# The down product of a row tile in one 512-column bank, and its adapter columns in a bank of their own

## What is computed

```python
def lora_add(base, inp, A, B):
    Ab = A[layer_idx][lora_indices]
    Bb = B[layer_idx][lora_indices]
    t = jnp.einsum('bri,bni->bnr', Ab, inp)
    return base + jnp.einsum('bor,bnr->bno', Bb, t) * SCALE
gate = lora_add(jnp.einsum('bnh,fh->bnf', x, W_gate), x, A_gate, B_gate)
up = lora_add(jnp.einsum('bnh,fh->bnf', x, W_up), x, A_up, B_up)
act = jax.nn.silu(gate) * up
down = lora_add(jnp.einsum('bnf,hf->bnh', act, W_down), act, A_down, B_down)
x = x + down          # H = 512, F = 1376
```

## Times and profile before

| | us |
|---|---|
| median of three runs | 654.25 |
| lowest, highest | 652.68, 658.75 |
| the profiled execution, from its first to its last instruction | 656.1 |

### The profile page before, as it was taken

The page is one execution under the profiler, slowest core; times in us unless marked ns, Lnnn a source line. Parts: engine busy times, 40 slices in busy tenths (PEclk is TensorE's granted clock), DMA queues, the critical chain, the costliest instruction groups (busy, mean ns, idle before and its releaser), DMA issues.

```text
span 656.1 us, 11454 instructions
## 1 busy us (share of the span) xinstructions
PE 615.8 (94%) x4659; PEld 599.5 (91%) x4659; DVE 300.1 (46%) x748; ACT 202.5 (31%) x514; POOL 210.0 (32%) x230
## 2 busy tenths in 40 slices
PE   4798998999999999999998999899987999999997
PEld 4797998999899899999998999899987998898985
DVE  3576543243333333333233323332331346889897
ACT  3464422231223122313231323132311333333331
POOL 4348341114111501151115111511164512656551
PEclk9899999999999989999999899999997999999998
DMA  6775042114212411141124011401134111131212
GB/s 201 251 257 160 30 136 85 39 34 131 75 39 65 126 47 39 65 141 33 39 65 157 17 39 65 157 17 39 33 129 129 39 33 49 50 97 65 96 49 81
DMA packets 26613, 55.80 MB, mean 85 GB/s; under 512 B 4224, under 2 KB 7744, under 8 KB 26560
## 3 DMA queue, kind: packets, MB, share of 16 engines
q1 hardware_dynamic: 18608, 31.17, 14.0%
q0 software_dynamic: 7808, 23.86, 12.0%
q10 hardware_dynamic: 144, 0.03, 0.0%
HBM read 46.66 MB, written 8.39 MB: 84 GB/s over the span
## 4 chain that ended last, share of the span: by engine, by line
PE 79%; DVE 9%; issue 6%; POOL 2%; ACT 1%; DMA 1%; SPq 1%; POOLq 0%; DVEq 0%; ACTq 0%
PE gu_ps L1031 15%; PE gu_ps L1030 15%; PE gu_ps L1029 15%; PE down_ps L1030 7%; PE down_ps L1029 7%; PE down_ps L1031 7%; DVE route L930 2%; PE l_ps L1031 2%; PE l_ps L1029 2%; PE l_ps L1030 2%; DVE x L948 1%; DVE wgu_sb L881 1%; POOL a_raw L563 1%; PE x2t_ps L1137 1%; PE tg_ps L1029 1%
## 5 line engine op out<-in xcount | busy, mean ns | idle before, releaser
L1029 PE MATMUL gu_ps<-xt,wgu_sb 128*128 128x256 f32 (+1 forms) x704 | 203.2, 289 | 9.3 <-DVE wgu_sb L881 8.3
L1031 PE MATMUL gu_ps<-xt,wgu_sb 128*128 128x256 f32 (+1 forms) x704 | 202.9, 288 | 5.0 <-issue 4.7
L1030 PE MATMUL gu_ps<-xt,wgu_sb 128*128 128x256 f32 (+1 forms) x704 | 202.5, 288 | 3.2 <-issue 3.1
L857 DVE TENSOR_TENSOR act<-act,gu_ps 128x256 f32<-128x256 f32 (+1 forms) x88 | 37.0, 420 | 243.2 <-ACT act L681 238.0
L1029 PEld LDWEIGHTS gu_ps<-xt,wgu_sb 128*128 128x128 f32 (+1 forms) x704 | 136.5, 194 | 11.6 <-DVE wgu_sb L881 8.3
L1031 PEld LDWEIGHTS gu_ps<-xt,wgu_sb 128*128 128x128 f32 (+1 forms) x704 | 136.8, 194 | 5.7 <-issue 5.7
L1030 PEld LDWEIGHTS gu_ps<-xt,wgu_sb 128*128 128x128 f32 (+1 forms) x704 | 136.5, 194 | 2.0 <-issue 2.0
L563 POOL DMA_INDIRECT b_sel_raw<-b_gu,idx_rank x48 | 46.2, 963 | 259.5 <-PE gu_ps L1031 243.6
L681 ACT ACTIVATE act<-gu_ps 128x256 f32<-128x256 f32 (+1 forms) x88 | 33.7, 383 | 289.8 <-PE gu_ps L1031 223.9
L1029 PE MATMUL down_ps<-wd_sb,act_hl 128*128 128x288 f32 (+1 forms) x352 | 104.8, 298 | 3.4 <-POOL wd_sb L625 1.9
L1031 PE MATMUL down_ps<-wd_sb,act_hl 128*128 128x288 f32 (+1 forms) x352 | 104.3, 296 | 2.8 <-issue 2.8
(11 more groups left out here) (132 smaller groups left out, 1019.1 us busy)
## 6 DMA issues: line engine op xcount, KB each, us to landing
wgu_sb_raw<-wgu SPq DMA_DIRECT2D x20, 256.0 KB, 5.2
xt_raw<-x_t SPq DMA_DIRECT2D x16, 256.0 KB, 3.1
x_res<-x_rows SPq DMA_DIRECT2D x8, 512.0 KB
x_after_l<-x_res SPq DMA_DIRECT2D x8, 512.0 KB
x<-x_after_l SPq DMA_DIRECT2D x16, 256.0 KB
out<-y SPq DMA_DIRECT2D x15, 256.0 KB, 2.1
wd_sb_raw<-wd SPq DMA_DIRECT2D x10, 256.0 KB, 5.6
w_raw<-w2ra_t SPq DMA_DIRECT2D x1, 1296.0 KB
```

The source lines that it names most:

```text
L857: ve.tensor_tensor(act[0:k, s % 2, :], act[0:k, s % 2, :], gu_ps[s % GU_BANKS][0:k, 1, :], ALU.mult).then_inc(s_mul, 1)
L1029: pe.matmul(out_, stationary[0], moving[0], start=start, stop=False, skip_group_check=True)
L1030: pe.matmul(out_, stationary[0], moving[1], start=False, stop=False, skip_group_check=True)
L1031: return pe.matmul(out_, stationary[1], moving[0], start=False, stop=stop, skip_group_check=True)
```

## The change

W_down's 512 columns of a chunk now lie together, and `down` makes one product with 512 moving columns for a row tile; `down_ps[q]` is one bank. The adapter columns have a tile of their own, `ad_sb` (for each chunk and row tile the 64 high columns, then the 64 low ones), and a bank of their own, `td_ps`. They are computed with two matmuls for a row tile: the high part of `act` by all 128 columns (high by high and high by low, which land in two column ranges), and the low part of `act` by the 64 high columns. `mask_td` masks both ranges and then adds them. `down_adapters` makes one product of 512 columns a row tile. A bank stays unused (`spare_ps`). On chip memory use is the same size.

```diff
-AD_HALF = TB * RANK // 2
-D_COLS = HALF + AD_HALF
+AD = TB * RANK
...
-        wd_sb, wd_sb_raw = sb_raw("wd_sb", [FC, 2, 2, AD_HALF + HALF + AD_HALF], mem_a)
+        wd_sb, wd_sb_raw = sb_raw("wd_sb", [FC, 2, H], mem_a)
+        ad_sb = sb("ad_sb", [FC, TILES, 2, AD], F32R, mem_a)
...
-        down_ps = [ps(f"down_ps{i}", [2, H], banks_a) for i in range(TILES)]
+        down_ps0 = ps("down_ps0", [H], banks_a)
+        td_ps = ps("td_ps", [TILES, 2, AD], banks_a)
+        down_ps = (down_ps0, ps("down_ps1", [H], banks_a))
+        ps("spare_ps", [H], banks_a)
...
-                w = slice(AD_HALF, AD_HALF + HALF)
-                return wd_sb_raw[0:k, c, 1, :, w], wd_sb[0:k, c, 0, :, w], wd_sb[0:k, c, 1, :, w]
+                return wd_sb_raw[0:k, c, 1, :], wd_sb[0:k, c, 0, :], wd_sb[0:k, c, 1, :]
...
-                for half in range(2):
-                    first = q * TB + half * TB // 2
-                    cols = slice(q * D_COLS, q * D_COLS + AD_HALF)
-                    raw = a_raw[:, first:first + TB // 2, 2 * A_GU + a * RANK:2 * A_GU + b * RANK]
-                    out.append((raw.rearrange("p b (c r) -> p c b r", r=RANK),
-                                *[wd_sb[:, a:b, part, half, cols].rearrange("p c (b r) -> p c b r", r=RANK)
-                                  for part in range(2)]))
+                raw = a_raw[:, q * TB:(q + 1) * TB, 2 * A_GU + a * RANK:2 * A_GU + b * RANK]
+                out.append((raw.rearrange("p b (c r) -> p c b r", r=RANK),
+                            *[ad_sb[:, a:b, q, part, :].rearrange("p c (b r) -> p c b r", r=RANK)
+                              for part in range(2)]))
...
+                own = const("scale_ch").unsqueeze(1).unsqueeze(3).to_broadcast([P, TILES, TB, RANK])
+                for part in range(2):
+                    ins = ve.tensor_tensor(td_parts(part).rearrange("p q (b r) -> p q b r", r=RANK),
+                                           td_ps[:, :, part, :].rearrange("p q (b r) -> p q b r", r=RANK),
+                                           own, ALU.mult)
+                ins.then_inc(s_tdp, 1)
+                ve.wait_ge(s_tdp, g + 1)
                 for q in range(TILES):
-                    own = slice(q * TB * RANK, (q + 1) * TB * RANK)
-                    ins = ve.tensor_tensor(
-                        td[:, q, own].rearrange("p (j b r) -> p j b r", j=2, r=RANK),
-                        td_of(q).rearrange("p j (b r) -> p j b r", r=RANK),
-                        const("scale_ch").rearrange("p (j b) -> p j b", j=2).unsqueeze(3).to_broadcast(
-                            [P, 2, TB // 2, RANK]), ALU.mult)
+                    ins = ve.tensor_tensor(td[:, q, q * AD:(q + 1) * AD], td_parts(0)[:, q, :],
+                                           td_parts(1)[:, q, :], ALU.add)
...
-                    at = q * AD_HALF
-                    for half in range(2):
-                        mm = product(down_ps[q][:, half, 0:D_COLS], a_hl,
-                                     [wd_sb[0:w, f, part, half, at:at + D_COLS] for part in range(2)], f == 0, False)
+                    product(down_ps[q][:], a_hl, [wd_sb[0:w, f, part, :] for part in range(2)], f == 0, False)
+                    pe.matmul(td_ps[:, q, :, :].rearrange("p k a -> p (k a)"), a_hl[0],
+                              ad_sb[0:w, f, q, :, :].rearrange("p k a -> p (k a)"), start=f == 0 and q == 0,
+                              stop=f == FC - 1, skip_group_check=True)
+                    mm = pe.matmul(td_ps[:, q, 0, :], a_hl[1], ad_sb[0:w, f, q, 0, :], start=False,
+                                   stop=f == FC - 1, skip_group_check=True)
...
-                    for half in range(2):
-                        cols = slice(half * HALF, (half + 1) * HALF)
-                        mm = product(down_of(q)[:, half, :], (td_hl[:, 0, rows], td_hl[:, 1, rows]),
-                                     (bd_hl[:, 0, cols], bd_hl[:, 1, cols]), False, True)
+                    mm = product(down_ps[q][:], (td_hl[:, 0, rows], td_hl[:, 1, rows]),
+                                 (bd_hl[:, 0, :], bd_hl[:, 1, :]), False, True)
```

More of the change, by code:

```diff
@@ L331, in bass_conditioned_residual_chain @@
         s_d = sem("s_d")
+        s_tdp = sem("s_tdp")
         s_dl = sem("s_dl")
@@ L439, in a_of @@
             for q in range(TILES):
-                for half in range(2):
-                    first = q * TB + half * TB // 2
-                    cols = slice(q * D_COLS, q * D_COLS + AD_HALF)
-                    raw = a_raw[:, first:first + TB // 2, 2 * A_GU + a * RANK:2 * A_GU + b * RANK]
-                    out.append((raw.rearrange("p b (c r) -> p c b r", r=RANK),
-                                *[wd_sb[:, a:b, part, half, cols].rearrange("p c (b r) -> p c b r", r=RANK)
-                                  for part in range(2)]))
-            return out
[L449 to L457, removed]
+                raw = a_raw[:, q * TB:(q + 1) * TB, 2 * A_GU + a * RANK:2 * A_GU + b * RANK]
+                out.append((raw.rearrange("p b (c r) -> p c b r", r=RANK),
+                            *[ad_sb[:, a:b, q, part, :].rearrange("p c (b r) -> p c b r", r=RANK)
+                              for part in range(2)]))
+            return out
         def w2_parts(n):
@@ L503, in load @@
                 elif kind == "wd":
-                    src = wd[it[1] * P:it[1] * P + cw(it[1]), :].rearrange("p (j n) -> p j n", n=HALF)
+                    src = wd[it[1] * P:it[1] * P + cw(it[1]), :]
                 else:
@@ L831, in mask_td, with td_parts @@
                     ve.wait_ge(s_tdt, g)
-                for q in range(TILES):
-                    own = slice(q * TB * RANK, (q + 1) * TB * RANK)
-                    ins = ve.tensor_tensor(
-                        td[:, q, own].rearrange("p (j b r) -> p j b r", j=2, r=RANK),
-                        td_of(q).rearrange("p j (b r) -> p j b r", r=RANK),
-                        const("scale_ch").rearrange("p (j b) -> p j b", j=2).unsqueeze(3).to_broadcast(
-                            [P, 2, TB // 2, RANK]), ALU.mult)
+                def td_parts(part):
+                    return t_raw[:, 0, part * P:(part + 1) * P].rearrange("p (q a) -> p q a", a=AD)
+                own = const("scale_ch").unsqueeze(1).unsqueeze(3).to_broadcast([P, TILES, TB, RANK])
[5 more added lines that the diff above has]
+                ve.wait_ge(s_tdp, g + 1)
+                for q in range(TILES):
+                    ins = ve.tensor_tensor(td[:, q, q * AD:(q + 1) * AD], td_parts(0)[:, q, :],
+                                           td_parts(1)[:, q, :], ALU.add)
                 ins.then_inc(s_mask, 1)
@@ L849, in job_lo @@
                         ve.wait_ge(s_dl, TILES * g + q + 1)
-                        x_q = x_res[:, q, :].rearrange("p (j n) -> p j n", n=HALF)
-                        ve.tensor_tensor(x_q, x_q, down_of(q), ALU.add).then_inc(s_x1, 1)
+                        ve.tensor_tensor(x_res[:, q, :], x_res[:, q, :], down_ps[q][:], ALU.add).then_inc(s_x1, 1)
                     return
```

## The result

The changed kernel takes 660.84 us (median of 8 runs, 660.12 to 663.17), the kernel before on the same chip 654.76 (8 runs, 652.68 to 658.75). The ratio is 1.0083 with a 95% interval of 1.0056 to 1.0110: slower by 0.8%, about 5 us, where 20 were forecast. The time lies just under the range. Both profiled executions are near each other too: a span of 658.3 us after, 656.1 before. (The one of before had its clock at the lower level more often, a mean granted clock of 0.980 for 0.995, so this difference of 2.2 is smaller than that of the medians.)

A forecast was written before the change was run, and what follows sets the result against it. TensorE was taken as the bound, by the distances between its instructions. 19.8 - 0.4 + 0.5 = +19.9 us took the span from 656.1 to 676.0 and the time from 654.25 to about 674, range 661 to 685.

The forecast's parts named there:

- number 6, the waits on issue: TensorE's 14.8 us of waits on issue, unexplained by the profile, were left as they are, bounds -3 and +3 us.
- The price of a narrow matmul: In down, 128- or 64-column matmuls cost their weight load, 111 ns each, 222 the pair (bounds 100 and 322); chance 0.70.
- loads go ahead: Rival: two weight loads fit under one 512-column matmul, a narrow pair costs 100 ns, about 654 us; chance 0.08.
- partly covered: Rival: loads start early, a narrow pair costs 161 ns, 664 us; chance 0.09, shared with partly absorbed.
- not overlapped: Rival: no load runs under a narrow matmul, a pair costs 322 ns, +16 us, 690 us; chance 0.13.
- Step 1, down,: Down matmuls of a row tile go from 795 to 917 ns, +0.244 us a step.
- Step 2, group 0 pays nothing: Group 0's seven down steps (1.7 us) disappear in 4.0 us of waits; the other 81 pay +19.8 us.
- step 5: Loads and splits of down weights and adapter pieces, and the residual addition: 0, bounds -0.5 and 0 us.
- Steps 3 and 4: Down adapters in 512-column products: -0.4 us; longer mask operations, hidden by slack except in the last group: +0.5 us.
- TensorE is not the bound in places: Rival: unnamed waits absorb 10 us of the extra, giving 664 us; chance 0.09, shared with partly covered.
- The sign named in the prediction: In the changed trace the first stage should end some 19 us later, the rest taking as long as before.

The follow-up runs named there:

- the repeat: The changed kernel, not altered, measured again on another chip against the kernel before: 662.39 us for 657.9, ratio 1.0080.

## Why the prediction was wrong

**The step that failed is number 6, the waits on issue.** It saw 14.8 us that it could not explain, found that a changed step has 40 instructions for 42 over a longer time, and still left the sum as it was, 3 either way, also for the clock. The runs show that the waits come with the gathers and that the change acts on them: it gave back about 10 us. Three kinds of kernel give the burst's price per group, from groups with and without gathers:

| matmuls of a down step | with gathers | without | a burst |
|---|---|---|---|
| 12 x 288 (before) | 64.90 | 61.58 | 3.3 |
| 6 x 512 and 4 narrow (after) | 65.11 | 64.00 | 1.1 |
| 12 x 256 and 4 narrow | 68.4 | 64.6 | 3.8 |

So the change gives back 2.2 us a group over the six bursts up to 460 us, 13 us. By the runs' ratios the gathers cost before 2.6% (17 us) and the changed kernel 1.2% (8 us), a difference of 10.

About half of that is the clock. In before's trace it fell for 3.4 us after three of the six bursts, by 1.8 us each 5.5 us in all, in after's after none. Before's two groups without such a stretch (63.8) put the burst by itself at 2.2 us, and the 256s come to about 2.0 if 1.8 is taken off their 3.8: an estimate from before's groups. So 512s halve a burst, 2.2 to 1.1, and in these executions they also kept the clock up. How often it falls differs between executions of the kernel before: on the chip of the repeat its 19 runs had mean granted clocks of 0.978 to 0.995 and took 661.1 to 652.7 us, the changed kernel's ten 0.992 to 0.995 and 661.0 to 664.8. At the same clock of 0.995 the one run of before (652.7) is 9.7 us under the changed kernel's median there, not 5.

**The price of a narrow matmul (the heart of the prediction) was right.** It is 0.22 us a pair, load-bound, and 64, 128 and 256 columns cost alike; the rivals *loads go ahead*, *partly covered* and *not overlapped* all fall with the two kernels that widen and omit them. By the Trainium skill (TensorE: Matmul & The Clock Gate, LDWEIGHTS) a load of 128 columns takes 107 ns; the rows' 0.11 agree. The 81 ns at 128 columns of the Trainium skill (TensorE: Matmul & The Clock Gate, Back-to-back issue gap) does not hold for these fp32r matmuls: they take 0.11 us.

**Step 1, down,** was slightly too large as a term: 0.22 us a step for 0.244 by the kernels without gathers, though the single step read 1.83 as forecast. Over 81 steps that is 2 us less, 18 in place of 19.8.

**Step 2, group 0 pays nothing,** holds, and more than that. The first `tg_ps` matmul of group 1, before and then after:

```profile
63.85 0.36 PE L1029 MATMUL tg_ps<-xt,agu_t 128*128 128x256 f32 x1 [1.11 <-DVE agu_t L881]
```

```profile
61.69 0.35 PE L1024 MATMUL tg_ps<-xt,agu_t 128*128 128x256 f32 x1 [0.97 <-DVE agu_t L876]
```

It is 2.2 us earlier, where step 5 allowed half a microsecond. The fewer and larger splits of an adapter piece save 0.3 to 0.4 (8 operations in 1.56 us on VectorE became 4 in 1.28, on ScalarE 1.59 became 1.21). TensorE's waits up to 66 us show where more of it lies: for VectorE's `t_hl` 0.8 us in place of 1.9, for GpSimd's low part of `wd_sb` 0.7 in place of 1.9. Why these became shorter was not found; this point moves by up to 2 us from kernel to kernel (62.4 to 64.1 in those built on before, 61.7 to 63.4 in those built on after). It stays open.

**Steps 3 and 4.** The down adapters can't be told apart from the rest. The mask and the transposes of the last group after the change, as the earlier trace rows:

```profile
547.22 0.49 DVE L827 TENSOR_TENSOR t_raw<-td_ps,const_sb 128x128 f32<-128x128 f32 x2 [2.26 <-PE td_ps L1093]
...
547.75 0.36 DVE L833 TENSOR_TENSOR td<-t_raw 128x64 f32<-128x64 f32 x2
...
548.16 0.44 PE L1102 MATMUL tg_ps<-const_sb,td 128*128 128x128 f32 x2
```

The two operations take 0.49 and the whole 0.89 us, as estimated (0.9), and no transpose waited for VectorE in the seven other groups. The half microsecond put down for the last group isn't to be seen: from the transposes to the end there are 110.1 us after (548.16 to 658.3) and 110.5 before (545.55 to 656.1).

**The sum again.** 20 were forecast, 5.4 came: 14.5 short. The bursts account for 10 of it, the smaller step for 2, the earlier start for 2 (in these two executions) and the mask for half a microsecond. No rival gave the measured time by its mechanism. *TensorE is not the bound in places* had 664, but the extra was not absorbed anywhere: all of it is paid (2.42 us a group without gathers), and something else became cheaper. The prediction also read a slow execution as a typical one: a span is about 2 us shorter than the time of its run (658.3 for 660.12 after), so the trace with a span of 656.1 belongs to a run some 4 us above the median of 654.25, in part by its three stretches at the lower clock. The sign named in the prediction, that the first stage ends 19 us later, was the one that failed: it ended 2.6 later (545.55 to 548.16 at the last transposes), though the single step took its 1.83.

**What stays open.** Shown is that bursts need the gathers, grow with the number of matmuls that carry the same columns (512s against 256s), and shrink when the gathers are paced. That TensorE's rate is then one of instructions and not of columns was seen for widths of 256 and 288 only. Not shown is what is shared inside: whether instruction fetch, the writing of descriptors or something else holds TensorE's instructions back. No run here separates these. The kept traces take away one form of the first: the queue that the page calls instruction brings packets of 16 KB (37 before, 35 after), one in 15 to 22 us, and none was under way in any of the six bursts of before or of after, nor landed at the end of one, so that no late packet of that queue ended them. Not tested is a longer burst that all kernels have (at about 487 to 500 us in before), with the weight gathers for the next stage (`w_raw`, eight in a row).

## What to carry to other kernels

Count weight loads and not columns: an fp32r matmul of 64 or 128 columns costs 0.11 us at the higher clock, about what one of 256 costs, so four narrow ones a step cost more than the wider products save. "Issue" waits are no constant to be carried over: look at which transfers they coincide with, and ask whether the change makes TensorE's instructions fewer and longer there, since that alone moved the time by 10 to 18 us here, about half of it by the clock. And where GpSimd issues gathers in a row beside a TensorE-bound loop, pace them: two a step for eight in a row gave 2.2% in the kernel before (1% in the changed one) without touching a matmul.

## What the runs showed of the hardware

- While GpSimd's gathers landed, TensorE started about 4 matmuls in a microsecond (8 of 256 columns elsewhere), at the higher clock, with no engine named as releaser. With 97 to 156 GB/s from GpSimd's queue alone it was 3 to 5. Transfers of the hardware queue at 215 to 291 GB/s without gathers left it at 10 in a microsecond.
- 3.4 us at the lower clock followed a burst in some cases: after each of six with 12 x 256, after three of six with 12 x 288 (but none of six in the run with the later residual load, though its bursts were longer), after none with 6 x 512 in `down` (one of six with the later load). A stretch cost about 1.8 us.
- A narrow matmul's recorded start misleads: 0.06 and 0.08 us to the next were recorded where 0.22 for the pair passed, and the matmul behind carries the rest in its duration.
